# Layer 0 attention: probabilities as the stationary operand, and output transposes in the score banks

## The reference, cut to what matters

```python
qkv = einsum('bsd,od->bso', x, w_qkv)          # 32 query heads, 8 key and value heads of 64
q, k = rms_norm(q, q_norm_w), rms_norm(k, k_norm_w)   # over 64, epsilon 1e-6
q, k = rope(q, k)
scores = einsum('bhqd,bhkd->bhqk', q, k_rep) / 8      # each key head serves 4 query heads
scores = scores + sliding_mask                        # causal, window of 64
probs = softmax(scores)
attn = einsum('bhqk,bhkd->bhqd', probs, v_rep)
out = einsum('bso,do->bsd', attn, w_out)
```

## Time and profile before

| | value |
|---|---|
| median of 3 runs | 1418.21 us (1415.92 to 1418.95) |
| profiled execution, its own time | 1424.83 us |
| its span | 1423.0 us, 28092 instructions |
| mean granted clock of PE | 0.932 |
| busy | PE 1188.3 us (84%), DVE 1075.8 (76%), POOL 664.8 (47%), ACT 650.0 (46%), PEld 681.4 (48%) |
| layer 0, steady part | 174.0 to 842.4 us |
| layer 1 | from about 915 us on |

### The profile page before, as it was taken

The page is one execution under the profiler, slowest core; times in us unless marked ns, Lnnn a source line. Parts: engine busy times, 40 slices in busy tenths (PEclk is TensorE's granted clock), DMA queues, the critical chain, the costliest instruction groups (busy, mean ns, idle before and its releaser), DMA issues. The chain is left out here.

```text
span 1423.0 us, 28092 instructions
## 1 busy us (share of the span) xinstructions
PE 1188.3 (84%) x9690; PEld 681.4 (48%) x9690; DVE 1075.8 (76%) x1925; ACT 650.0 (46%) x1424; POOL 664.8 (47%) x1051
## 2 busy tenths in 40 slices
PE   0499988997988988888888889726899999999998
PEld 0266655664665655655655556413433333333334
DVE  1799987878777878788778787636688888877751
ACT  1144432333323323333333333210399999987884
POOL 1477765656655757566567566440133333211000
PEclk9999998989989999989989999955799999999999
DMA  4200001101101111011011011140000000000000
GB/s 177 99 12 18 20 13 29 31 13 28 30 13 20 26 26 20 19 33 21 19 32 21 12 29 21 27 129 26 1 2 2 2 2 2 2 10 9 13 6 30
DMA packets 108892, 37.26 MB, mean 26 GB/s; under 512 B 93312, under 2 KB 107600, under 8 KB 108240
## 3 DMA queue, kind: packets, MB, share of 16 engines
q1 hardware_dynamic: 108752, 35.46, 10.1%
HBM read 18.77 MB, written 4.19 MB: 16 GB/s over the span
## 5 line engine op out<-in xcount | busy, mean ns | idle before, releaser
L1090 DVE TENSOR_REDUCE l_mxv<-l_mx 128x1 f32<-128x1024 f32 x256 | 306.4, 1221 | 66.5 <-PE l_mx L1276 63.3
L978 ACT ACTIVATE l_prob<-l_sc 128x512 f32<-128x512 f32 x512 | 285.9, 597 | 48.8 <-PE l_sc L1283 46.2
L578 POOL TENSOR_TENSOR t<-t 128x320 f32<-128x320 f32 x128 | 110.3, 862 | 287.4 <-DVE t L465 257.9
L512 DVE RECIPROCAL rc<-pv 128x256 f32<-128x256 f32 x128 | 223.4, 1746 | 4.1 <-PE pv L720 4.1
L1276 PE MATMUL l_mx<-l_kt,l_qt 48*128 48x512 f16 x512 | 179.3, 396 | 8.6 <-DVE l_mxv L1090 6.9
L1283 PE MATMUL l_sc<-l_qt,l_kt 50*128 50x512 f16 x512 | 177.2, 386 | 0.0
L325 ACT ACTIVATE kts<-tr 128x256 f16<-128x256 f16 x128 | 49.0, 383 | 252.2 <-DVE kts L478 252.2
L1256 PE MATMUL l_acc<-l_prob,qkv_all 128*17 128x256 f32 x2048 | 161.4, 388 | 0.1
L736 PE MATMUL ob<-wo,ats 128*128 128x256 f32 x512 | 160.7, 441 | 0.8 <-DVE ats L515 0.8
L1143 POOL TENSOR_SCALAR l_mxs<-l_mxv 128x8 f32<-128x8 f32 x32 | 7.5, 233 | 322.7 <-DVE l_mxv L1090 322.7
L569 POOL TENSOR_TENSOR rm<-ve,half_neg 128x5 f32<-128x5 f32 x128 | 151.5, 1183 | 0.1
(11 more groups left out here) (179 smaller groups left out, 2490.7 us busy)
## 6 DMA issues: line engine op xcount, KB each, us to landing
qkv_all<-qs SPq DMA_DIRECT2D x16, 256.0 KB, 4.0
v<-v SPq DMA_DIRECT2D x240, 16.0 KB, 1.8
qkv_all<-w_qkv SPq DMA_DIRECT2D x1, 3072.0 KB, 10.5
xn_all<-xs SPq DMA_DIRECT2D x16, 128.5 KB, 2.0
wo<-w_o SPq DMA_DIRECT2D x1, 2048.0 KB, 13.2
xa<-x SPq DMA_DIRECT2D x16, 128.0 KB, 2.8
xc<-x SPq DMA_DIRECT2D x16, 128.0 KB, 2.3
out<-xc SPq DMA_DIRECT2D x16, 128.0 KB, 2.0
```

What stands on the lines that cost most here:

```text
L512: dve.reciprocal(rc[:, :, :], pv[:, 256:512].rearrange("p (j t) -> p j t", j=2)).then_inc(s_["dve_rc"], 1)
L578: pool.tensor_tensor(t1[:, b, :, :], t1[:, b, :, :], t2[:, :, :], ALU.add).then_inc(s_["pool_u"], 1)
L978: act.activation(prob[:, (y * NI + u) % NPR, h * 512:(h + 1) * 512], sc[:, k % NSC, :], ACT.Exp, scale=D1 ** -0.5).then_inc(s_["act_sc"], 1)
L1090: dve.tensor_reduce(mxv[:, x % 2, u:u + 1], mx[:, MX[k] % 2, :], AX.X, ALU.max).then_inc(s_["dve_mx"], 1)
```

## The change

- **Value products.** The probabilities become the stationary operand (128 keys x 128, two heads of 64 queries) and the values move, 65 columns wide: `v0` and `v1` get a column of ones, so the 65th column of the result is the sum. Four f32 products in place of eight. The result stands by queries on partitions (`pvv`), no longer transposed.
- **Reciprocals.** DVE takes the reciprocal of 4 columns and multiplies 4 x 64 columns by it, broadcast, into `an`.
- **Output transposes.** A new step with `LAG_O` 9: behind the projection PE transposes `an` (two f32 transposes) into columns 256 to 383 of the two score banks (`atv`). For this it waits for DVE's `an`, for the exponential of the slot before, and for ACT's evacuation of the transposes before. ACT evacuates them into `ats`, ahead of the square, and the output product waits for that.
- **Order on PE.** The first four score products stand behind the value products and wait also for the evacuation; the last two stand behind the output product.
- **Epsilon.** The squares have one more column per head, the 65th, that holds the epsilon; the sum over 65 takes it in, and the addition goes.
- **Keys.** `nat` holds the key once, high and low. PE transposes each half twice, to both halves of the output partitions, with half-width weights: four small transposes in place of two whole ones. DVE's copy goes, and POOL makes the low parts in one instruction.

```diff
...
 LAG_V = 8
+LAG_O = 9
 LAG_W = 9
...
         xl = sb("xl", [P, 2, KC, B, P], F16)
-        sq = sb("sq", [P, NH, HD])
+        sq = sb("sq", [P, NH, HD + 1])
         ss = sb("ss", [P, 2, NH])
-        ve = sb("ve", [P, 2, NH])
         rm = sb("rm", [P, 2, NH])
...
         t2 = sb("t2", [P, NH, HD])
-        nat = sb("nat", [P, 2, REP + 2, P], F16)
+        nat = sb("nat", [P, 2, NH, P], F16)
         qt = sb("qt", [P, 2, REP, P], F16)
         kts = sb("kts", [P, B, 2, G, WIN + P], F16)
-        v0 = sb("v0", [P, B, G, HD])
-        v1 = sb("v1", [P, B, G, HD])
+        v0 = sb("v0", [P, B, G, HD + 1])
+        v1 = sb("v1", [P, B, G, HD + 1])
         pm = sb("probs", [P, 2, 2, REP, WIN])
...
         ht = sb("ht", [P, NF, B, P])
-        rc = sb("rc", [P, 2, P])
-        ats = sb("ats", [P, 2, 2, P])
+        rc = sb("rc", [P, 2, 4])
+        an = sb("an", [P, 2, 2, 2, HD])
+        ats = sb("ats", [P, 2, 2, 2, WIN])
         st2 = sb("st2", [P, 2, 6])
...
         pv = ps("pv", [P, 512])
-        pvo, pvs = (pv[:, j * 256:(j + 1) * 256].rearrange("p (j h q) -> p j h q", j=2, h=2) for j in range(2))
+        pvv = pv[:, 0:4 * (HD + 1)].rearrange("p (a d) -> p a d", a=4)
+        atv = sc[:, :, 256:384].rearrange("p h (a q) -> p h a q", a=2)
         ob = ps("ob", [P, 512])
...
                     ev(qs[:, h * W1C:(h + 1) * W1C], extra[:, 0:W1C]).then_inc(s_["act_l1"], 1)
+                n, k, ok = at(s, LAG_O)
+                b = k % 2
+                if ok:
+                    act.wait_ge(s_["pe_O"], n * G + k + 1)
+                    wait(act, s_["pe_W"], n * G + k - 1)
+                    ev(ats[:, b, :, :, :].rearrange("p a h q -> p h a q"), atv).then_inc(s_["act_at"], 1)
                 n, k, ok = at(s, LAG_A)
...
                     wait(act, s_["dve_ss"], n * G + k)
-                    act.activation(sq[:, :, :], qk[:, 0:NH * HD], ACT.Square, scale=1.0 / 8).then_inc(s_["act_sq"], 1)
+                    act.activation(sq[:, :, 0:HD], qk[:, 0:NH * HD].rearrange("p (h d) -> p h d", h=NH), ACT.Square, scale=1.0 / 8).then_inc(s_["act_sq"], 1)
                     if n >= B:
...
                         act.wait_ge(vnw[k], (n - 1) * 16)
-                    ev(v1[:, n % B, k, :], qk[:, NH * HD:CW], 1.0 / WS).then_inc(s_["act_A"], 1)
+                    else:
+                        act.wait_ge(s_["set_pool"], 1)
+                    ev(v1[:, n % B, k, 0:HD], qk[:, NH * HD:CW], 1.0 / WS).then_inc(s_["act_A"], 1)
                 n, k, ok = at(s, LAG_N)
...
                     wait(act, s_["pe_T"], n * G + k - 1)
-                    ev(nat[:, b, 0:NH, 0:HD], t1[:, b, :, :]).then_inc(s_["act_hi"], 1)
+                    ev(nat[:, b, :, 0:HD], t1[:, b, :, :]).then_inc(s_["act_hi"], 1)
                 c = (s - LAG_F0) % 16 // 2
...
             dve.memset(half_neg[:, :], -0.5)
-            link(dve.memset(one[:, :], 1.0))
+            dve.memset(sq[:, :, HD:HD + 1], WS * WS * RMS_EPS)
             dve.wait_ge(ld[1], 16)
...
                     dve.wait_ge(s_["act_sq"], n * G + k + 1)
+                    wait(dve, s_["pool_rm"], n * G + k - 1)
                     dve.tensor_reduce(ss[:, b, :], sq[:, :, :], AX.X, ALU.add).then_inc(s_["dve_ss"], 1)
-                    dve.wait_ge(s_["dve_ss"], n * G + k + 1)
-                    wait(dve, s_["pool_rm"], n * G + k - 1)
-                    dve.tensor_scalar(ve[:, b, :], ss[:, b, :], WS * WS * RMS_EPS, None, ALU.add).then_inc(s_["dve_ve"], 1)
                 n, k, ok = at(s, LAG_T)
...
                                              ALU.mult).then_inc(s_["dve_h"], 1)
-                n, k, ok = at(s, LAG_N)
-                b = k % 2
-                if ok:
-
-                    dve.wait_ge(s_["act_hi"], n * G + k + 1)
-                    wait(dve, s_["pe_T"], n * G + k - 1)
-                    dve.tensor_copy(nat[:, b, REP, HD:P], nat[:, b, REP, 0:HD]).then_inc(s_["dve_dup"], 1)
                 n, k, ok = at(s, LAG_T)
...
                     dve.wait_ge(s_["pe_V"], n * G + k + 1)
-                    wait(dve, s_["dve_an"], n * G + k)
-                    dve.reciprocal(rc[:, :, :], pv[:, 256:512].rearrange("p (j t) -> p j t", j=2)).then_inc(s_["dve_rc"], 1)
+                    wait(dve, s_["dve_an"], n * G + k - 1)
+                    dve.reciprocal(rc[:, b, :], pvv[:, :, HD]).then_inc(s_["dve_rc"], 1)
                     dve.wait_ge(s_["dve_rc"], n * G + k + 1)
-                    wait(dve, s_["pe_W"], n * G + k - 1)
-                    dve.tensor_tensor(ats[:, b, :, :], pv[:, 0:256].rearrange("p (j t) -> p j t", j=2), rc[:, :, :], ALU.mult
-                                      ).then_inc(s_["dve_an"], 1)
+                    wait(dve, s_["pe_O"], n * G + k - 1)
+                    dve.tensor_tensor(an[:, b, :, :, :].rearrange("p h a d -> p (h a) d"), pvv[:, :, 0:HD],
+                                      rc[:, b, :].unsqueeze(2).broadcast_to([P, 4, HD]), ALU.mult).then_inc(s_["dve_an"], 1)
                 n = pair_tile(s + 3)
...
             pool.memset(kts[:, :, :, :, :], 0.0)
-            pool.memset(nat[:, :, REP + 1, HD:P], 0.0)
-            pool.memset(v0[:, :, :, :], 0.0).then_inc(s_["set_pool"], 1)
+            pool.memset(v0[:, :, :, :], 0.0)
+            pool.memset(v1[:, :, :, :], 1.0).then_inc(s_["set_pool"], 1)
             pool.wait_ge(ld[2], 16 * 3 * NH)
...
                     wait(pool, s_["pe_T"], n * G + k - 1)
-                    pool.tensor_tensor(nat[:, b, 0:REP, HD:P], t1[:, b, 0:REP, :], nat[:, b, 0:REP, 0:HD], ALU.subtract)
-                    pool.tensor_tensor(nat[:, b, REP + 1, 0:HD], t1[:, b, REP, :], nat[:, b, REP, 0:HD],
-                                       ALU.subtract).then_inc(s_["pool_lo"], 1)
+                    pool.tensor_tensor(nat[:, b, :, HD:P], t1[:, b, :, :], nat[:, b, :, 0:HD], ALU.subtract
+                                       ).then_inc(s_["pool_lo"], 1)
                 n, k, ok = at(s, LAG_A)
...
-                    pool.wait_ge(s_["dve_ve"], n * G + k + 1)
-                    rsqrt(rm[:, b, :], ve[:, b, :], NH).then_inc(s_["pool_rm"], 1)
+                    pool.wait_ge(s_["dve_ss"], n * G + k + 1)
+                    rsqrt(rm[:, b, :], ss[:, b, :], NH).then_inc(s_["pool_rm"], 1)
                     pool.wait_ge(s_["pool_rm"], n * G + k + 1)
...
                     ins.then_inc(s_["pe_A"], 1)
+                n, k, ok = at(s, LAG_O)
+                b = k % 2
+                if ok:
+                    pe.wait_ge(s_["dve_an"], n * G + k + 1)
+                    t, j, ahead = at(s, LAG_S + 1)
+                    if ahead:
+                        pe.wait_ge(s_["act_exp"], t * G + j + 1)
+                    wait(pe, s_["act_at"], n * G + k)
+                    for h in range(2):
+                        ins = pe.transpose(atv[:, h, :, :], an[:, b, h, :, :], idf[:, :])
+                    ins.then_inc(s_["pe_O"], 1)
                 f = (s - LAG_F0) % 16 // 2
...
                 if ok:
-                    pe.wait_ge(s_["dve_dup"], n * G + k + 1)
                     pe.wait_ge(s_["pool_lo"], n * G + k + 1)
                     wait(pe, s_["dve_qt"], n * G + k)
-                    for j in range(REP + 2):
-                        ins = pe.transpose(tr[:, j, :], nat[:, b, j, :], idh[:, :])
+                    for j in range(REP):
+                        pe.transpose(tr[:, j, :], nat[:, b, j, :], idh[:, :])
+                    for j in range(2):
+                        for a in range(2):
+                            ins = pe.transpose(tr[a * HD:(a + 1) * HD, REP + j, :], nat[:, b, REP, j * HD:(j + 1) * HD],
+                                               idh[:, :])
                     ins.then_inc(s_["pe_T"], 1)
-                n, k, ok = at(s, LAG_S)
-                if ok:
-                    pe.wait_ge(s_["dve_qt"], n * G + k + 1)
-                    wait(pe, s_["act_exp"], n * G + k)
-                    pe.matmul(weights[0], keys(n, k, 1, 0, top), queries(k, 0, top), start=True, stop=False)
-                    pe.matmul(weights[1], outside(n, 1), eyes, start=True, stop=False)
-                    pe.matmul(weights[0], keys(n, k, 0, 0, full), queries(k, 0, full), start=False, stop=False)
-                    pe.matmul(weights[1], keys(n, k, 0, 1, full), queries(k, 1, full), start=False, stop=False
-                              ).then_inc(s_["pe_S1"], 1)
                 n, k, ok = at(s, LAG_V)
...
                         for a in range(2):
-                            pe.matmul(pvo[a * HD:(a + 1) * HD, :, h, :], v[:, bb, k, :], pm[:, b, h, 2 * a:2 * a + 2, :],
-                                      start=True, stop=True)
-                    for h in range(2):
-                        for a in range(2):
-                            ins = pe.matmul(pvs[a * HD:(a + 1) * HD, :, h, :], one[:, :], pm[:, b, h, 2 * a:2 * a + 2, :],
+                            ins = pe.matmul(pvv[:, 2 * h + a, :], pm[:, b, h, 2 * a:2 * a + 2, :], v[:, bb, k, :],
```

(24 more changed lines are left out.)

7 lines of the change are left out of this document (3 added, 4 removed).

## The result

The changed kernel takes 1431.57 us (median of 5 runs, 1429.44 to 1434.90), the kernel before, run beside it, 1418.95 (5 runs, 1415.92 to 1424.05): ratio 1.0088, interval [1.0059, 1.0118], so 0.9% or 12.6 us slower. The forecast was 1416. The profiled execution after took 1431.57 us (span 1429.7), the one before 1424.8 (span 1423.0), so the two traces show 6.7 of the 12.6 us, because before's profiled execution is one of its slower ones.

The account below looks back on a forecast made before the run. It took the kernel as an alternation of two nearly equal engines, PE and DVE, with PE waiting 87 of 668 us. PE's work +46, waits -48 and clock 0 gave -2 on 1418.2: 1416 us, range 1380 to 1446.

Parts of the forecast that it names:

- the clock: PE's granted clock, 0.93 in the stretch: effects behind the two once-per-tile stalls taken as cancelling, 0 us, bounds -30 and +25.
- (a): Once per tile DVE stands at L547 for PE's transposes of the next slot: 53.5 us, 12 times.
- PE, +0.36 a slot, +46: PE's added work over 128 slots: value products, output transposes, half-width key transposes, two more shape changes; bounds -0.1 to +0.8.
- This stands in every slot, also in the early ones: PE's +0.36 us a slot holds in early slots too, where waits are few; early tiles longer by about 3.
- Waits, -48: PE's idle: 28.8 us before value products and 14 before the projection go, some 5 more after 842.4 us.
- (b): Once per tile, carried value rows queue behind stores in SP's queue, delaying PE's projection; its 14 us of waiting would go.
- DVE near 290: DVE sheds about 2.56 us a slot; its 532 busy us in 96 slots fall to some 290, no longer the bound.
- New waits: Possible waits for the exponential, ACT's evacuation and SP: nothing expected; at most 0.4 us for evacuation, some tenths at SP.
- the even trade: The forecast case: PE's added work and its lost waits balance, -2 us, own range 1400 to 1430; chance 0.40.
- Rival B: Layer 0: PE's clock comes back as idle shrinks, 94 us at 1.2 GHz become about 45; 1388 us; chance 0.27.
- Rival C: Output transposes: PE is the bound and the 28.8 us of waits return there; +27, 1445 us; chance 0.22.
- Rival D: Value products: weight loads are not hidden, 1.3 us a slot, +51, 1467 us, perhaps 1455; chance 0.06.

Follow-up runs that it names:

- after_wholekey: The changed kernel with the six whole f16 transposes of before, DVE's key copy and GpSimd's two subtractions back: 1424.85 us, 1.0036 of the kernel before.
- pad128: The changed kernel with the eight value products moving 128 columns in place of 65, results placed 128 columns apart: 1401.69 us, 0.9885 of the kernel before.
- after_O2: The changed kernel with PE making its two f32 output transposes twice: 1442.94 us, 1.0177 of the kernel before.
- before_key: The kernel before with only the keys held once and transposed twice at half width: 1422.74 us, ratio 1.0035.
- before_T2: The kernel before with PE making its four query transposes twice: 1419.49 us, ratio 0.9985.
- before_scr_sp: The kernel before with L547 writing a tile of its own and SP's stores of the rotated qkv two slots later: 1323.86 us.
- before_eps: The kernel before with only the epsilon as a 65th summed column: 1417.92 us, ratio 1.0003.

## Why the prediction was wrong

The step that failed is the clock: "I take these as cancelling: 0, bounds -30 [...] and +25." The change added 40 us at 1.2 GHz by the profiled executions; at the two prices found above, 0.34 and 0.49 us per us, that is 14 to 20 us in place of 0 (an estimate; the prices count the waits that follow too). The prediction had named the sign's reason ("thinner work behind them (transposes, 65-column products)") and then put nothing for it. The two stalls from which it read the clock were the wrong place to look: the slots behind (a) hardly changed (10.3 to 10.8 us), and its row for them was the shortest of the twelve.

What the traces show in its place is the drain. It had no step of its own in the sum: its slots were counted among the 128 at +0.36 each, and it took 7.5 us more, with 42 us at 1.2 GHz in place of 17. In the drain PE has no projections any more, and transposes, 65-column products, scores and output products are left. That its length goes with the clock is shown by four traces of the changed kernel and its variants: 62.1 us at a clock of 0.66 (after), 60.8 at 0.67 (after_wholekey), 56.2 at 0.87 (pad128), 55.2 at 0.92 (after_O2). Up to the last projection the changed kernel was 4.0 us faster, and layer 1's 3.2 us are not the change's: over the 17 kernels traced it takes 477 to 484 us with the same code, 482.5 in after, but also 482 to 483 in before_key, before_T2 and before_scr_sp, and 479.5 in after_wholekey.

The clock is not the whole of the 12.6 us. The half-width key transposes, a PE cost that the sum had at 0.06 us a slot, account for 6.7 of them by their removal; since the clock did not rise with it, and the wide products left 5.0 of it, that saving is one of PE's work. With them gone the kernel is still some 5 us slower than before, at before's pace on PE in a plain slot, with less on DVE and at the lowest clock.

The other steps:
- *PE, +0.36 a slot, +46*: +0.25 in a plain slot; PE's busy time up to the last projection rose by 36 us (32 of them in the twelve tiles), part of which is the lower clock. The value products took 1.03, not 0.90, but the "two more" changes of shape cost nothing: after_wholekey has them all and the plain slot of before. What cost was the item put at 0.06, the half-width key transposes: 0.21 by the starts, 0.26 with what follows (0.12 in before_key).
- *"This stands in every slot, also in the early ones"*: wrong. The second and third early tiles took 41.35 and 43.68 us against 41.61 and 43.83, so not 3 us more but a little less: plain slots there are longer by some 0.26 too, but PE's idle time in the first 120 us fell by as much as its work rose (8.6 to 4.1 us).
- *Waits, -48*: PE's idle time up to the last projection fell by 40 us. In the twelve tiles the three waits of the sum gave 26 of the 43 put there, two that it had not listed gave 10, and 1.6 for GpSimd's low parts are new. The value products' wait went, as put. The wait before the output transposes came out 5 us over the 26.9 that it was to keep. The 14 us of (b) did not go: the projection's wait stands 20 times, 29.1 us. Three slots longer by 0.25 (or less, where they wait too) don't cover 1.14 us.
- *DVE near 290*: 357. The 517 ns of the epsilon addition were mostly a wait for GpSimd, which moved to the next copy; before_eps shows it alone.
- *New waits*: none for the exponential, for ACT's evacuation or for SP in the rows, as put.

Two errors nearly cancelled each other: PE's work was put at +46 and rose by 36, the idle time at -48 and fell by 40. So that the time up to the last projection came out near the even trade, -4.0 us against -2, is in part luck, the more so as it holds 10 us more at 1.2 GHz. Rival B had the clock as what decides, with the opposite sign: it "comes back" only once (a) and (b) themselves are gone, or with wider products. Rival C had the sign and the neighbourhood but the wrong mechanism: the waits before the output transposes rose by 5 us, not by 29. Rival D is refuted by the 1.03 us.

What stays open: why PE's clock falls in one drain and not in another. Narrow value products alone don't do it (after_O2). No run alters the drain alone, and of each kernel only one drain was traced. The price of PE's work by itself is open too, since every run that added work also moved the clock.

## What to carry to other kernels

An even trade of work between two engines is worth what the stalls leave of it: find the once-per-tile stalls first (a scratch output that aliases a buffer in use, a store ahead of a load in a queue); here they were worth 76 to 80 us (one) and 93 to 133 (both), and decided whether the change cost 12.6 or gained 25. Where the profile shows part of a stretch at the lower clock, do not put the clock's term at nothing: give it bounds on the side that the new work points to, read it from all slots of a kind and not from one, and count the drain as a stage of its own. Before an operation is removed for its measured duration, look whether that duration is its own or a wait that the next one will take over.
